# A convolution block and a test-time-training scan on one core: z products and scores in one product, head pairs in the K and Q transfer, and new orders

## What is computed

```
x = x + conv3x3( relu( gn(x) * mask(gn(x)) ) ) + bias        # gn: group norm over groups of 4 channels
x = x + ttt( layer_norm( tokens( gn(x) ) ) )                 # 784 tokens of 128 channels per image

ttt:   XQ, XK = rope(heads(xn @ q_w.T)), rope(heads(xn @ k_w.T));  XV = heads(xn @ v_w.T)   # 8 heads of 16
       eta    = token_idx * sigmoid(xn . lr_w + lr_b) / 16
       for each chunk of 16 tokens, in sequence, with state W1c (16 x 16 per head and image), b1c:
           Z1     = xk @ W1c + b1c
           grad   = backward of a layer norm with an L2 loss (Z1, target xv - xk)
           Attn1  = tril(xq @ xk.T)
           Z1_bar = xq @ W1c - et * Attn1 @ grad + (b1c - tril(et) @ grad)
           W1c    = W1c - (last_eta * xk).T @ grad ;   b1c = b1c - sum(last_eta * grad)
           out    = xq + layer_norm(Z1_bar)
       y = layer_norm(out) @ o_w.T
```

## Time and profile before

| | |
|---|---|
| median of 3 runs | 1983.95 us (1970.23 to 1985.82) |
| the profiled execution | 1980.83 us, its span 1979.0 us |
| instructions | 82050 |
| PE busy, PE weight loads busy | 1626.2 us (82%), 1208.9 us (61%) |
| DVE, ACT, POOL busy | 1518.3 (77%), 1017.6 (51%), 1316.5 us (67%) |
| mean granted TensorE clock | 0.638 of full speed |

### The profile page before, as it was taken

One profiled execution on the slowest core, in us unless ns is written; L12 is line 12 of the kernel. 1 busy time (PEld: TensorE's weight loads), 2 busy tenths in 40 slices (PEclk: granted clock), 3 DMA queues, 4 the chain that ended last, 5 costly groups with the idle time before them and its releaser, 6 DMA issues.

```text
span 1979.0 us, 82050 instructions
## 1 busy us (share of the span) xinstructions
PE 1626.2 (82%) x33524; PEld 1208.9 (61%) x33524; DVE 1518.3 (77%) x3567; ACT 1017.6 (51%) x2487; POOL 1316.5 (67%) x1480
## 2 busy tenths in 40 slices
PE   4778898903888888988988888889889888888886
PEld 2444454501776766766766767767667666666674
DVE  6987766604888878888888888888888887888864
ACT  3434656542555555555555555555555555555543
POOL 2263535474778777777777777777777777777753
PEclk9899999955556555556565655555655666555555
DMA  6077698963457566666665665665666665656554
GB/s 239 1 39 60 99 85 69 81 165 46 61 69 80 67 71 75 71 74 71 72 77 69 74 76 66 75 78 68 74 73 73 74 73 68 77 66 75 66 60 49
DMA packets 1650519, 148.82 MB, mean 75 GB/s; under 512 B 1630176, under 2 KB 1643744, under 8 KB 1650144
## 3 DMA queue, kind: packets, MB, share of 16 engines
q1 hardware_dynamic: 1390640, 117.87, 51.1%
q10 hardware_dynamic: 259504, 25.70, 10.8%
HBM read 40.71 MB, written 38.54 MB: 40 GB/s over the span
## 4 chain that ended last, share of the span: by engine, by line
SPq 23%; PE 17%; DVE 16%; DMA 9%; issue 8%; ACT 3%; DVEq 0%; POOL 0%; ACTq 0%; POOLq 0%
SPq L479 16%; DMA kqk<-work 8%; SPq L495 6%; PE p_kt L1641 6%; PE p_x L1685 4%; DVE work L1315 2%; DVE work L1282 2%; DVE work L1306 2%; PE p_m L1670 2%; DVE work L1375 1%; PE p_x L1676 1%; DMA late<-work 1%; DVE zs L1362 1%; DVE m L1369 1%; DVE work L1397 1%
## 5 line engine op out<-in xcount | busy, mean ns | idle before, releaser
L816 ACT ACTIVATE work<-p_kt 128x512 f16<-128x512 f32 x196 | 148.2, 756 | 215.3 <-PE p_kt L1641 215.2
L1641 PEld LDWEIGHTS p_kt<-fold,kqk 128*128 128x128 f16 x6272 | 184.9, 104 | 98.4 <-ACT work L816 47.2
L1641 PE MATMUL p_kt<-fold,kqk 128*128 128x16 f16 x6272 | 201.1, 175 | 53.0 <-DMA kqk<-work 43.6
L1614 PE MATMUL p_j<-wa,work 128*128 128x512 f16 x196 | 119.5, 610 | 148.0 <-DVE work L1282 103.0
L626 POOL TENSOR_TENSOR work<-work,rope_s 128x256 f32<-128x256 f32 x196 | 160.9, 841 | 85.5 <-DVE work L1282 85.5
L597 POOL TENSOR_TENSOR work<-work,g 128x256 f32<-128x256 f32 x98 | 71.7, 732 | 206.0 <-DVE work L1353 203.2
L1544 PE MATMUL p_j<-work 128*128 128x392 f16 x864 | 158.5, 344 | 30.7 <-POOL work L540 18.3
L1315 DVE TENSOR_TENSOR work<-work 128x256 f16<-128x256 f32 x196 | 162.0, 880 | 15.8 <-ACT work L803 15.8
L1685 PEld LDWEIGHTS p_y<-w,late 128*128 128x128 f16 x4704 | 146.6, 104 | 19.6 <-issue 9.7
L1685 PEld LDWEIGHTS p_x<-w,late 128*128 128x128 f16 x4704 | 148.9, 105 | 12.3
L1614 PEld LDWEIGHTS p_j<-wa,work 128*128 128x128 f16 x196 | 24.9, 127 | 208.3 <-issue 177.4
(11 more groups left out here) (174 smaller groups left out, 4438.5 us busy)
## 6 DMA issues: line engine op xcount, KB each, us to landing
kqk<-work SPq DMA_DIRECT2D x392, 64.0 KB, 4.7
late<-work SPq DMA_DIRECT2D x392, 64.0 KB, 3.7
late<-work SPq DMA_DIRECT2D x392, 32.0 KB, 2.5
out_y<-work ACTq DMA_DIRECT2D x49, 256.0 KB, 6.8
x_scratch<-late SPq DMA_DIRECT2D x24, 392.0 KB, 11.7
xs_scratch<-work SPq DMA_DIRECT2D x24, 392.0 KB, 6.5
work<-x_scratch ACTq DMA_DIRECT2D x49, 192.0 KB, 3.7
work<-xs_scratch SPq DMA_DIRECT2D x48, 192.0 KB, 2.9
```

The costliest lines, as they stand in the source:

```text
L816: return act.activation(kqt16[:, o, g:g + GP, :, :, :].rearrange("p g h t a -> p g a (h t)"), p_kt[:, :].rearrange("p (g a n) -> p g a n", ...
L1614: pe.matmul(p_j[k][:, 0:4 * C], tokens(s, k, 0), wa16[:, :], start=True, stop=False, skip_group_check=True)
L1641: mm = pe.matmul(p_kt[:, at:at + CS], part_of(g + k, h, a), fold16[:, :], start=True, stop=True)
```

## The change

- **z and scores in one product.** `k_dot_q` is gone. `z_state` now makes its 48 products with 32 moving columns instead of 16: 16 columns of the state (`w16`) and 16 of the transposed Q (`kqt16`), which for that end lie in one tile `wq16`. The scores of a slot land in the second half of bank `p_x[p]`. So `m_mask`, `m_high` and `m_low` are done per slot on 256 columns (98 each) instead of per chunk on 512 (49 each).
- The gradient's products leave that half of the bank for a bank of their own, `p_g` (once `p_m`), and `rate_project` moves into the second half of `p_y`.
- **K and Q as head pairs.** `hl16` and `kqk` interleave two heads, so a run of `kq_spread` is 128 bytes instead of 64 and each of its 8 transfers has 16 x 32 runs instead of 16 x 64, with the same bytes. The stationary operands of `fold_k`, `fold_q` and `grad` are read from there with a step of 4 elements of float16 (8 bytes) instead of 2.
- **New scan order** in `turn(k)` of all five engines. `m_spread` needs `m_low` of both slots.
- **Second norm spread.** `gn_mean` of the second norm is issued after the second half of image 8q + 1, and `gn_var`, `gn_root` and `gn_scale` go to image 8q + 2; `scaled_at` starts one image later and scales two images beside each of three convolutions instead of two.
- Small tables are moved so that `work` fits in 12616 words.

```diff
-LEAD = 4
+LEAD = 3
...
-        w16 = sb("w16", [128, GP, 2, 2, SC], F16)
+        wq16 = sb("wq16", [128, 4 * GP * SC + 2 * NG * C * 2], F16)
+        w16 = wq16[:, 0:4 * GP * SC].rearrange("p (k c n a) -> p k c n a", k=GP, c=2, a=2)
+        kqt16 = wq16[:, 4 * GP * SC:].rearrange("p (o g h t a) -> p o g h t a", o=2, g=NG, h=NH, a=2)
...
-        blocks = kqk[:, :].rearrange("p (o g h b d a) -> p o g h b d a", o=3, g=NG, h=NH, b=GB, a=2)
+        blocks = kqk[:, :].rearrange("p (o s b d a j) -> p o s b d a j", o=3, s=NG * HP, b=GB, a=2, j=2)
...
-            q, i = (b - 2) // GB - 1, (b - 2) % GB
-            if q < 0 or i > 5:
+            q, i = (b - 3) // GB - 1, (b - 3) % GB
+            if q < 0 or i > 4:
...
-                part = hl16[:, c % 2, :, :, :, :].rearrange("p o g (h d) a -> p (o g h) (d a)", d=HD)
+                part = hl16[:, c % 2, :, :, :, :, :].rearrange("p o s d a j -> p (o s) (d a j)")
...
             def m_spread(c):
-                sp.wait_ge(m_low_done.sem, m_low_done.count(c))
-                sp.wait_ge(m_high_done.sem, m_high_done.count(c))
+                sp.wait_ge(m_low_done.sem, m_low_done.count(2 * c + 1))
+                sp.wait_ge(m_high_done.sem, m_high_done.count(2 * c + 1))
...
             def turn(k):
-                kq_spread(k - 3)
                 m_spread(k - 4)
+                turned_spread(k - 3)
                 xs_next(k)
-                turned_spread(k - 3)
+                kq_spread(k - 2)
...
-            @guard_chunk
-            def k_dot_q(c):
-                pe.wait_ge(turned_landed.sem(c), turned_landed.count(c))
-                pe.wait_ge(rate_scaled_done.sem, rate_scaled_done.count(min(c + LEAD // 2 - 1, NCH - 1)))
-                if c >= 1:
-                    pe.wait_ge(m_low_done.sem, m_low_done.count(c - 1))
-                for g in range(NG):
-                    for h in range(NH):
-                        at = g * C + h * CS
-                        for j, (a, w) in enumerate(HL):
-                            mm = pe.matmul(p_m[:, at:at + CS], kq_turned(c, 1, g, h, a), kqt16[:, 0, g, h, :, w],
-                                           start=(j == 0), stop=(j == 2))
-                mm.then_inc(k_dot_q_done.sem, 1)
...
+            @guard
+            def z_state(s):
+                c, p = s // 2, s % 2
+                pe.wait_ge(turned_landed.sem(c), turned_landed.count(c))
+                if s >= 2:
+                    pe.wait_ge(w_low_done.sem, w_low_done.count(s - 2))
+                    pe.wait_ge(b_low_done.sem, b_low_done.count(s - 2))
+                    pe.wait_ge(m_low_done.sem, m_low_done.count(s - 2))
+                    pe.wait_ge(z_hat_done.sem, z_hat_done.count(s - 2))
+                with_bias(p_x[p][:, 0:SC], s)
+                both = p_x[p][:, :].rearrange("p (o n) -> p o n", o=2)
+                for k in range(GP):
+                    for h in range(NH):
+                        at = slice(k * C + h * HD, k * C + (h + 1) * HD)
+                        for j, (a, w) in enumerate(HL):
+                            mm = pe.matmul(both[:, :, at], kq_turned(c, 1, GP * p + k, h, a), state_and_q(s, k, h, w),
+                                           start=False, stop=(j == 2), skip_group_check=True)
+                mm.then_inc(z_done.sem, 1)
```

More of the change, by code:

```diff
@@ L22 @@
 GP = 2
+HP = NH // 2
 NS = NCH * GP
@@ L306, in program @@
         qt_copy_done = step("qt_copy")
-        k_dot_q_done = step("k_dot_q")
         m_mask_done = step("m_mask")
@@ L686, in turn @@
                 g_scaled(2 * k - 3)
-            for k in range(NCH + 4):
+                g_hat(2 * k - 3)
+                g_dot(2 * k - 3)
+                rope_sin(2 * k + 1)
+                o_scaled(2 * k - 5)
+                rope_sum(2 * k + 1)
+                g_both(2 * k - 3)
+                o_sum_q(2 * k - 5)
+                q_out(2 * k + 1)
+            for k in range(NCH + 3):
                 turn(k)
@@ L802, in qk_high @@
                     at = o if c % 2 == 1 else 1 - o
-                    last = act.activation(hl16[:, c % 2, at, g:g + GP, :, 0], pair(qk[:, o, :]), ACT.Copy)
+                    last = act.activation(half_of(c, at, g, 0), split(qk[:, o, :]), ACT.Copy)
                 last.then_inc(qk_high_done.sem, 1)
@@ L1472, in turn @@
             def turn(k):
+                o_sum(2 * k - 8)
+                o_inverse(2 * k - 8)
+                o_hat(2 * k - 8)
+                final(2 * k - 10)
+                w_step(2 * k - 7)
+                norm(2 * k - 2)
+                rope_cos(2 * k - 2)
+                z_sum(2 * k - 6)
+                m_mask(2 * k - 6)
+                z_inverse(2 * k - 6)
+                z_hat(2 * k - 6)
+                m_mask(2 * k - 5)
+                z_sum(2 * k - 5)
+                z_rate(2 * k - 6)
@@ new lines, in turn @@
+                m_low(2 * k - 6)
+                z_inverse(2 * k - 5)
+                post_stats(2 * k - 8)
+                post_aggr(2 * k - 8)
+                g_means(2 * k - 6)
+                g_along(2 * k - 6)
+                z_hat(2 * k - 5)
+                o_sum(2 * k - 7)
+                m_low(2 * k - 5)
+                g_centre(2 * k - 6)
+                qk_low(2 * k - 2)
+                post_inverse(2 * k - 8)
+                g_rated(2 * k - 6)
+                ln_inverse(2 * k - 1)
@@ new lines, in turn @@
+                o_inverse(2 * k - 7)
+                norm(2 * k - 1)
+                z_rate(2 * k - 5)
+                b_step(2 * k - 6)
+                o_hat(2 * k - 7)
+                final(2 * k - 9)
+                rope_cos(2 * k - 1)
+                g_means(2 * k - 5)
+                g_low(2 * k - 6)
+                g_along(2 * k - 5)
+                g_centre(2 * k - 5)
+                rate_scaled(k - 1)
+                w_step(2 * k - 6)
+                g_rated(2 * k - 5)
+                post_stats(2 * k - 7)
```

319 lines of the change are left out of this document (136 added, 183 removed).

## The result

| | median of the runs, us | profiled execution: time (span) |
|---|---|---|
| before | 1981.5 (1970.2 to 1985.8) | 1980.8 (1979.0) |
| after | 2070.3 (2064.9 to 2079.6) | 2064.9 (2063.1) |

The ratio is 1.048 (95% interval 1.044 to 1.051): slower by 4.8%, where 1915 us was forecast. Forecast and result are 155 us apart, or 3.2 us a turn.

The account below looks back on a forecast made before the run. A loop through several engines, not one full engine, was taken to set the 30.2 us turn; the scores loop, longest at 28.8, saves 48 turns x 1.4 = 67 us from 1980.8, giving 1915 us, range 1855 to 1995.

Parts of the forecast that it names:

- The store: y_store issued earlier, close behind the copy, sharing DMA with nearly all of turned_spread: 8.9 us, and 3.8 to land.
- The spread of K and Q: kq_spread with half the runs: 6.4 us issuing plus 2.5 landing, instead of 9.74 + 2.84, 3.7 us less.
- loop A: The scan's K and Q loop: kq_spread, landing, folds and copies, turned_spread, xs_next; 30.6 us before, 27.8 forecast.
- `xs_next`: Load on SP put behind turned_spread: its 1.4 us leave the scores' loop and stay in the K and Q loop.
- loop B: The scan's scores loop: z_state to m_spread, m_spread, turned_spread, landing, next z_state; 30.1 us before, 28.8 forecast, the longest.
- The stretch of the folds: First fold to turned_spread, four folds and copies: left at 8.55 us, bounds 1 us either way.
- The step of 8 bytes: Stationary operands of folds and grad on TensorE: no cost taken, upper bound 6.0 us a turn.
- Scores per slot: From z_state to m_spread, with the odd slot's m_low late in DVE's list: 9.6 us instead of 7.88.
- 32 columns: Joined z and scores product on TensorE: extra columns cost nothing, upper bound 1.2 us a turn.
- the odd `z_state`: Ahead of the first fold, it finds w_low of the slot before hardly done: no stall taken, upper bound 1 us.
- The second norm: First stage, scaled_at an image later: taken as 0, bounds 5 us less and 8 us more.
- The slower rival: Scores take the K and Q spread's place, in the scores loop at 31.15 us: 46 us more, 2027 us; chance 0.11.

Follow-up runs that it names:

- `xs_mid`: The changed kernel with xs_next(k-1) ahead of m_spread(k-4) in SP's turn, no longer between turned_spread and kq_spread: 2000.8 us, ratio 1.012.

## Why the prediction was wrong, step by step

- **The store (the step that failed).** "ACT's new list brings it close behind the copy, so that its 256 KB share the DMA engines with nearly all of `turned_spread` ... I take 8.9, near the upper one." The mechanism was seen and its size missed. The 9.29 us that I took for the upper end was a long turn of a spread with a median of 7.8, of which only the last third overlapped the store; with the overlap nearly whole the median was 10.9 us, and even with the store cut to one image it was 8.9. The term was 2.0 us a turn too low, in both loops, 48 x 2.0 = 96 us of the 155. Moving the store alone returned 104 us.
- **The spread of K and Q.** 6.4 + 2.5 = 8.9 was nearly right (5.66 + 2.49 in one turn, 5.9 + 3.3 = 9.2 by the medians). But the 9.74 + 2.84 that it replaced were not the price of 64-byte runs alone: with the store cut to one image the same spread of the kernel before has a median of 7.5 us instead of 10.1. In the kernel before the longer runs alone gave 8 us, where loop A was to lose 3.7 us a turn.
- **`xs_next`.** It was priced at 1.4 us, its row in the place where it stood before. Behind `turned_spread` it and its gaps take 2.51 (median 2.3). With this, the folds and the landing, loop A, which I had 1.0 us under loop B, was the longer one. Moving it away gave 71 us.
- **The stretch of the folds.** 8.55 with a bound of 1 us either way; 9.59 was measured. With a step of 4 bytes it was 8.80, so 0.8 us of it is the step and what `project` added is small. Both hold over the turns (medians 9.6 and 8.8).
- **The step of 8 bytes.** Taken as nothing, bound 6.0 us; measured 1.55 us of TensorE a turn, 29 us in the time. The rule that I drew on, the Trainium skill, "SBUF — State Buffer", "Door 1: The DMA port swizzle" (two hits in a line keep full bandwidth), doesn't hold for these reads (38.4 ns a fold product against 31.6 with a step of 4 bytes): the measurement decides.
- **Scores per slot.** 9.6 forecast, 10.19 measured (median 11.1), `m_spread` itself 5.31 instead of 6.4. That the sum is right within 0.5 us in the turn read is partly luck: I let DVE's list set `m_low`, but it waited for ACT's `m_high`, which stood behind a `kt_copy` that waited for the first fold. Where that fold comes earlier, in `xs_mid`, the stretch has a median of 9.7 us, so DVE's path was priced well and did not decide. The rest of loop B's surplus came from `turned_spread` and the wait for the copies.
- **32 columns, the odd `z_state`, DVE.** As forecast or nearly: 1.6 ns a product, no stall (in the turn read the odd `z_state` follows the even one without a hole), and DVE at 0% of the chain.
- **The second norm.** Taken as 0. SP's last stores of the first stage ended at 397.8 instead of 406.3 us, and the first `m_spread` came 6.0 us earlier: a small gain inside my bounds.

The slower rival named the place rightly (long transfers in loop B), but with other causes and 46 us instead of 89. What I did not do was to ask of each duration of before what stood beside it: the store made `kq_spread` long there (medians 10.1 us with it and 7.5 without). Priced without it, the change had little to win, and its new place for the store was a loss in the longest transfer of both loops. Of the 95 us between the kernels the store's place explains about half (104 - 52 = 52 us by the two runs that move it, 42 by the two that cut it). With the store and `xs_next` moved the changed order comes to 0.975 and the order before, with its store moved, to 0.974: the rest of the change is worth nothing that can be told.

## What to carry to other kernels

Before a transfer's duration goes into a sum, look what runs beside it, and read it in many turns: one turn had 9.29 us where the median was 7.8. Cut or move the neighbour to see what it adds, in both kernels that are compared. Large stores that nobody waits for belong where the issuing queue of the loop stands still, and a step's place in a list is not its place in time, so look at both. A step that is moved takes its waits along: they, and the queue behind them, decide more than its own length.
